# Two PSUM tiles in place of one for the gate and up products of a quantized feed-forward layer

## The reference

```python
def _weight_quant(w):
    scale = 1.0 / jnp.clip(jnp.mean(jnp.abs(w)), 1e-05)
    return jnp.clip(jnp.round(w * scale), -1.0, 1.0) / scale
def _act_quant(x):
    scale = 127.0 / jnp.clip(jnp.max(jnp.abs(x), axis=-1, keepdims=True), 1e-05)
    return jnp.clip(jnp.round(x * scale), -128.0, 127.0) / scale
def _bitlinear(x, w):
    return jnp.einsum('bsi,oi->bso', _act_quant(x), _weight_quant(w))
gate = jax.nn.silu(_bitlinear(x, w_gate))
up = _bitlinear(x, w_up)
return _bitlinear(gate * up, w_down)      # inner width 4096
```

## Time and profile before

| | us |
|---|---|
| median of 3 runs | 5976.22 (5973.66 to 5980.92) |
| profiled execution, its own time | 5984.42 |
| its span, the slowest core (6) | 5982.5 |
| fastest core of that execution (3) | 5927.1 |
| busy on core 6: TensorE | 2458.8 (41%) |
| VectorE | 2156.1 (36%) |
| ScalarE | 1436.4 (24%) |

### The profile page before, as it was taken

How to read it: one execution, slowest core, us unless ns; L and a number is a source line. 1 busy time by engine, 2 the same in 40 slices (tenths; PEclk the granted TensorE clock), 3 DMA queues, 4 the chain that set the end, 5 groups by cost and what they waited for, 6 DMA issues and landing times.

```text
span 5982.5 us, 37845 instructions; the slowest of 8 cores (5927.1 to 5982.5 us)
## 1 busy us (share of the span) xinstructions
PE 2458.8 (41%) x10934; PEld 1088.1 (18%) x10934; DVE 2156.1 (36%) x4980; ACT 1436.4 (24%) x2000; POOL 294.7 (5%) x487
## 2 busy tenths in 40 slices
PE   0000444444442444444442464345462555335563
PEld 0000222222221222222221121012110121011111
DVE  4544444444444444444443222222313222222312
ACT  0000444444442444444442220002100120002100
POOL 0001000000000000000000001100010001100010
PEclk9999666666665666666665765568755675568656
DMA  7766000000003000000001112211131111312131
GB/s 247 286 215 168 22 22 16 22 22 16 22 15 74 22 16 22 22 16 22 22 13 55 59 57 71 74 56 56 49 97 53 61 60 53 86 48 70 34 99 48
DMA packets 201146, 371.58 MB, mean 62 GB/s; under 512 B 127216, under 2 KB 135408, under 8 KB 193776
## 3 DMA queue, kind: packets, MB, share of 16 engines
q0 software_dynamic: 67056, 230.72, 12.5%
q1 hardware_dynamic: 133888, 138.43, 8.2%
HBM read 314.58 MB, written 41.94 MB: 60 GB/s over the span
## 4 chain that ended last, share of the span: by engine, by line
PE 28%; DVE 25%; DMA 23%; ACT 14%; issue 9%; DVEq 1%; SPq 0%; ACTq 0%; POOLq 0%; POOL 0%
DMA wdslab<-wdq_s 6%; PE pd L1138 5%; PE pd L1332 4%; PE pd L1144 4%; DMA wslab<-wgq_s 3%; PE ps_f L490 3%; DMA wslab<-wuq_s 3%; ACT L740 3%; DVE tmpu L634 2%; ACT L1156 2%; DVE s1b L651 2%; DVE s1f L648 1%; DVE tmpu L639 1%; PE pd L1485 1%; ACT L519 1%
## 5 line engine op out<-in xcount | busy, mean ns | idle before, releaser
L1138 PE MATMUL pd<-xqTg,wslab 128*128 128x512 bf16 x1024 | 373.8, 531 | 599.0 <-DVE guT L1174 289.4
L1332 PE MATMUL pd<-wdslab,gcvt 128*128 128x512 bf16 x1024 | 450.0, 593 | 359.2 <-DMA wdslab<-wdq_s 232.7
L490 PE MATMUL ps_f<-wf_b,xnT 128*128 128x512 bf16 x512 | 227.3, 624 | 735.5 <-DVE s2b L661 513.9
L1174 DVE TENSOR_TENSOR guT<-pd,sgT 128x512 f32<-128x512 f32 x128 | 88.5, 692 | 894.4 <-ACT sgT L1156 894.4
L1156 ACT ACT_TABLE_LOAD x128 | 164.2, 1283 | 959.4 <-PE pd L1144 959.4
L441 ACT ACT_TABLE_LOAD x64 | 82.1, 1283 | 1131.3 <-DVE lncol L434 1131.3
L827 ACT ACT_TABLE_LOAD x128 | 164.2, 1283 | 625.2 <-DVE eok L819 625.2
L1144 PE MATMUL pd<-xqTg,wslab 128*128 128x512 bf16 x1024 | 301.3, 447 | 0.0
L1320 DVE CAST gcvt<-guqT 128x256 bf16<-128x256 int8 x256 | 74.4, 293 | 588.2 <-PE pd L1332 588.2
L1138 PEld LDWEIGHTS pd<-xqTg,wslab 128*128 128x128 bf16 x1024 | 117.0, 123 | 831.4 <-issue 806.5
L762 PE MATMUL ps_m<-identb,qtb 128*128 128x128 bf16 x256 | 47.5, 288 | 535.0 <-DVE qtb L750 535.0
(11 more groups left out here) (188 smaller groups left out, 4995.1 us busy)
## 6 DMA issues: line engine op xcount, KB each, us to landing
wdslab<-wdq_s POOLq DMA_DIRECT2D x256, 256.0 KB, 2.9
wtmp<-wgT SPq DMA_DIRECT2D x16, 2048.0 KB, 10.6
wtmp<-wuT SPq DMA_DIRECT2D x16, 2048.0 KB, 10.6
wtmp<-wdT SPq DMA_DIRECT2D x64, 512.0 KB, 4.0
xin<-x POOLq DMA_DIRECT2D x64, 512.0 KB, 5.0
wslab<-wgq_s POOLq DMA_DIRECT2D x32, 1024.0 KB, 6.1
wslab<-wuq_s POOLq DMA_DIRECT2D x32, 1024.0 KB, 6.1
wgq_s<-wqb POOLq DMA_DIRECT2D x8, 1024.0 KB, 14.8
```

The costliest lines, as they stand in the source:

```text
L490: i = t.matmul(out=dst_ps[:], lhsT=xnTs(dc), rhs=wsb[:, dc * 512:(dc + 1) * 512], start=(dc == 0), stop=(dc == 7))
L1138: i = t.matmul(out=pd[0][:, 0:512], lhsT=wslab[:, gbase + dc * 512 + isl * 128: gbase + dc * 512 + (isl + 1) * 128], rhs=xqTg[:, dc * GTOK ...
L1174: i = v.tensor_tensor(out=guT[:, sl_id * GTOK:(sl_id + 1) * GTOK], in0=pd[0][:, 512:1024], in1=sgT[:], op=ALU.mult)
L1332: i = t.matmul(out=pd[sg * 2 + bi2][:, half * 512:(half + 1) * 512], lhsT=gcvt[:, ppd * 256 + bi2 * 128: ppd * 256 + (bi2 + 1) * 128], rhs ...
```

## The change

TensorE's slices alternate between `pd[0]` and `pd[1]`, and `sgT` has two halves in the same alternation. TensorE waits for the product of the slice before the last instead of that of the last. The buffer `mxT` becomes another name of `sabs`. No instruction is added, dropped or put in another place on any engine: the programs are the same row for row but for the tiles' addresses and the value of one wait.

```diff
--- before.py
+++ after.py
@@ -958,10 +958,10 @@
         guT = sb("guT", [128, 32 * GTOK], F32)
         guqT = sb("guqT", [128, 32 * GTOK], I8)
         gcvt = sb("gcvt", [128, 2 * 256], BF16)
-        sgT = sb("sgT", [128, GTOK], F32)
+        sgT = sb("sgT", [128, 2 * GTOK], F32)
         sabs = sb("sabs", [128, GTOK], F32)
         mxM = [sb("mxM0", [128, GTOK], F32), sb("mxM1", [128, GTOK], F32)]
-        mxT = sb("mxT", [128, GTOK], F32)
+        mxT = sabs
         colmax = sb("colmax", [128, 4], F32)
         fcol = sb("fcol", [128, 16], F32)
         qrow = sb("qrow", [1, GTOK], F32R)
@@ -1125,23 +1125,26 @@
                 for isl in range(4):
                     sl_id = ic * 4 + isl
 
+                    pdg = pd[sl_id % 2]
+                    sgs = (sl_id % 2) * GTOK
+
                     @block.tensor
                     def _(t, pp=pp, isl=isl, mk_slab=mk_slab, mk_xqT=mk_xqT,
-                          sl_id=sl_id):
+                          sl_id=sl_id, pdg=pdg):
                         S.wait(t, f"qg{pp}", mk_slab)
                         S.wait(t, "qt0", mk_xqT)
-                        if prod_marks:
-                            S.wait(t, "dv", prod_marks[-1])
+                        if len(prod_marks) >= 2:
+                            S.wait(t, "dv", prod_marks[-2])
                         gbase = (pp * 2 + 0) * 4096
                         ubase = (pp * 2 + 1) * 4096
                         for dc in range(8):
-                            i = t.matmul(out=pd[0][:, 0:512],
+                            i = t.matmul(out=pdg[:, 0:512],
                                          lhsT=wslab[:, gbase + dc * 512 + isl * 128:
                                                     gbase + dc * 512 + (isl + 1) * 128],
                                          rhs=xqTg[:, dc * GTOK:(dc + 1) * GTOK],
                                          start=(dc == 0), stop=(dc == 7))
                         for dc in range(8):
-                            i = t.matmul(out=pd[0][:, 512:1024],
+                            i = t.matmul(out=pdg[:, 512:1024],
                                          lhsT=wslab[:, ubase + dc * 512 + isl * 128:
                                                     ubase + dc * 512 + (isl + 1) * 128],
                                          rhs=xqTg[:, dc * GTOK:(dc + 1) * GTOK],
@@ -1151,10 +1154,10 @@
                     mk_gu = S.val("pe")
 
                     @block.scalar
-                    def _(sc, mk_gu=mk_gu):
+                    def _(sc, mk_gu=mk_gu, pdg=pdg, sgs=sgs):
                         S.wait(sc, "pe", mk_gu)
-                        i = sc.activation(out=sgT[:], in_=pd[0][:, 0:512], func=AF.Silu,
-                                          scale=inv_swg[:])
+                        i = sc.activation(out=sgT[:, sgs:sgs + GTOK], in_=pdg[:, 0:512],
+                                          func=AF.Silu, scale=inv_swg[:])
                         S.inc(i, "sc")
                     mk_sg = S.val("sc")
 
@@ -1162,17 +1165,17 @@
                         @block.gpsimd
                         def _(g, mk_sg=mk_sg):
                             S.wait(g, "sc", mk_sg)
-                            g.dma_start(out=dbg_aps["d_sg"], in_=sgT[:]
+                            g.dma_start(out=dbg_aps["d_sg"], in_=sgT[:, 0:GTOK]
                                         ).then_inc(S.h["qst"], 16)
                         S.c["qst"] += 16
 
                     @block.vector
-                    def _(v, sl_id=sl_id, mk_sg=mk_sg):
+                    def _(v, sl_id=sl_id, mk_sg=mk_sg, pdg=pdg, sgs=sgs):
                         S.wait(v, "sc", mk_sg)
                         if grp == 0 and sl_id == 0 and "d_sg" in dbg_aps:
                             S.wait(v, "qst", S.val("qst"))
                         i = v.tensor_tensor(out=guT[:, sl_id * GTOK:(sl_id + 1) * GTOK],
-                                            in0=pd[0][:, 512:1024], in1=sgT[:],
+                                            in0=pdg[:, 512:1024], in1=sgT[:, sgs:sgs + GTOK],
                                             op=ALU.mult)
                         S.inc(i, "dv")
                     prod_marks.append(S.val("dv"))
```

## The result

The changed kernel takes 5690.87 us (median of 8 runs, 5687.23 to 5698.06), the kernel before, run beside it, 5963.93 us (8 runs, 5956.58 to 5980.92). The ratio is 0.9539, with a 95% interval from 0.9527 to 0.9551: 273 us less. The forecast was 5712 us, 5670 to 5765. The profiled execution of the changed kernel took 5690.6 us; that of the kernel before took 5984.4, above all eight of these runs and 20 us over their median.

The account below looks back on a forecast made before the run. No engine fills the gate and up stages; a serial chain with 68 on-path product waits bounds them. Terms -205.4 - 73 + 6 + 8 = -264.4 take 5984.4 to 5720.0 us, 5712 as a median; range 5670 to 5765.

Parts of the forecast that it names:

- The path: Gate and up stages: 68 waits for the product lie on the path; the next slab's two loads hide the others.
- The term of -205.4: Gate and up stages: all 68 on-path waits for the product go, -205.4 us.
- The later slices: 68 slices behind on-path waits: shorter without clock drops, -73 us, bounds -98.0 (clock 1.0) and -47.7 (0.81).
- The middle between 1.0 and 0.81: Later slices: -73 us, taken midway between all at clock 1.0 and all at 0.81.
- the rival without the limit: No peak-current limit, so all later slices run at clock 1.0: -98.0 us for them, 5687 us in all; chance 0.10.
- The rival with the limit everywhere: A peak-current limit holds every later slice at clock 0.81: 5737 us; chance 0.25.
- First slices and tails: Slabs' 32 first slices start with the clock down, +6 us; 28 tails, holding the next slab's two loads, +8.
- the rivals with longer loads: Slab loads slow down when asked for sooner: 5858 us without loss, chance 0.05; 6199 us, slower than before, 0.03.
- One sign that the prediction set for being wrong: Slab tails, third slice's end to next slab: the prediction is wrong if one passes 15.7 us.
- Edits at nothing: Doubled `sgT`, `mxT` in the buffer of `sabs`, and first writes to `pd[1]`: no added wait, no cost.
- The longer reads that were bounded at +36: ScalarE and VectorE reading PSUM slower beside TensorE's writes: 36 slices late, 0 to +36 us, taken as 0.

Follow-up runs that it names:

- the old wait: Changed kernel, but TensorE again waits for the product of the slice just before: 5965.09 us, ratio 1.0002 against the kernel before.
- fillers: Kernel before, with 12 extra unread matmuls on TensorE behind each slab's first three slices: 5921.96 us, ratio 0.9914.
- the loads issued early: Kernel before, one PSUM tile, with a slab's loads issued as soon as their buffer is free: 5818.51 us, ratio 0.9745.
- early loads: Changed kernel, two tiles, slab loads issued once their buffer is free: 5344.36 us; also with both halves issued one right behind the other: 5327.11 us.
- The slow silu: Changed kernel with the silu made three times over, so each product comes later: 5726.34 us, ratio 0.959 against the kernel before.

## Why the prediction was right, and where its sizes were not

*The path.* That 68 of the 96 waits count, and that the load behind the third slice hides the rest, held: the old wait undoes the whole gain, fillers give back the clock alone, and with the loads issued early 124 waits count instead, so that the second tile is worth 474 us. The term of -205.4 was measured as such, on core 6 and on core 0.

*The later slices.* On core 6 this is the term that was mis-sized: -73 forecast, -97.1 measured, next to its bound of -98.0. The middle between 1.0 and 0.81 was wrong: each of the 68 slices ran at 1.00, on core 6 and on the five other cores whose matmul records are complete. On core 0 the same term is -71, and that this is close to -73 is luck. The forecast left room for the 0.81 after the change, where it did not come, and took its base of 331.95 from the core that had most of it before; on cores 0, 1 and 3 that base is 285 to 306.

What came is the rival without the limit, given a chance of 0.10: its condition holds, and its 5687 us is nearer to 5690.87 than the forecast of 5712. That it fits so well is luck as well, since its sum starts from the same execution, with first slices and tails taken 19 us too dear on core 6. The rival with the limit everywhere (5737) did not come. Denser matmuls on all cores did not bring the 0.81 to any core of the changed kernel's trace, nor with early loads, where TensorE is busy for nearly the whole stage at 0.98 of 2.4 GHz.

The Trainium skill's page "TensorE: Matmul & The Clock Gate", section "Seeing it yourself", has a die held at 13/16 of the clock while several of its cores run dense matmuls; these traces show a clock of that size, but not with the density: 0.81 for 269 us of core 6's stages before and for none after. The section "A second HAM failure mode: psum-queue depth-cycling" of the same page of the Trainium skill has the clock fall back between groups of matmuls that cycle through PSUM banks. This trace does not show it: TensorE alternates between two tiles, and 68 of 68 later slices stand at 1.00, with no idle time at the hand-over.

*First slices and tails* were taken 5 and 14 us too dear on core 6; on core 0 they came out at +5 and +2 where +6 and +8 were forecast. The loads are not slower for being asked for sooner: a tail is 14.01 us on average, before 14.24, and a load of L1117 lands after 6.1 us (median; 8.2 at most), before 6.1 and 8.7. That answers the rivals with longer loads. One sign that the prediction set for being wrong did come: a tail of 17.10 us, above 15.7. The sign was a poor one, read from core 6 alone; on core 1 of the kernel before one tail took 17.92.

*The end.* The forecast is 21 us above the median. Of these, 12 are its start: the sum began at an execution 20 us over the median of its runs, and the 8.2 us to the median known then were too little to take off. The other 9 are the change, 273 against 264. That it is so near rests on two errors that met, the 0.81 counted in the base and half of it left in the forecast. Core 6 shows neither number: its stage shrank by 43 us more than forecast, and the rest of its program took 13.8 us longer. This rest moved by -18 to +14 us over the six cores, so the stage and not the span of one core is what the terms can be held against.

*Edits at nothing.* The longer reads that were bounded at +36 did not come: the product took 0.69 us beside TensorE's writes. The slow silu's 35 us for a product later by 1.6 shows what the bound would have meant. Its 32 waits are four fewer than the 36 counted, since a late third slice leaves the last slab's fourth on time.

## What to carry to other kernels

A second buffer is worth the waits that lie on the path, not those that the profile counts; look for what else ends late in the same loop, here a load that was issued three slices after its buffer was free. Once that is put right, the same second buffer is worth 1.7 times as much, so the two edits are better judged together. A pause of TensorE can be paid for twice, in the wait and in the slower matmuls behind it: a slice after a 3.0 us wait took up to 6.6 us where one without took 3.6; after waits of 1.0 us none ran at 1.2 GHz. And before a term is priced on the slowest core, look at the granted clock of the others: what is peculiar to one execution of that core goes into the base of every term.

No run shortened the wait itself. 1.28 of its 3.0 us is a table load ahead of each silu, 128 in all, though ScalarE runs only table loads and silus in these stages; what leaving them out would give is not shown.

## What the runs showed of the hardware

The granted clock of 0.81 came by die, and without following how dense the matmuls were. In the profile of the kernel before all four cores of the second die had it, for 210 to 295 us of their spans, and none of the first; with fillers all four of the first die, for 136 to 310 us, and none of the second. In the changed kernel no core of the profile had it, nor in the far denser kernels with early loads and two tiles. What calls for it stays open; no run here was made to find out.
